# Windowed differential attention in a fused eight-layer kernel: fewer steps ahead of the unit loop, the rest as one piece per unit, and the copy of PV's result one unit later

## What is computed

```python
q = q * cos + rotate_half(q) * sin          # 16 heads
k = k * cos + rotate_half(k) * sin          # 4 heads, repeated 4 times
q1, q2 = (q[..., :SUB], q[..., SUB:])
k1, k2 = (k[..., :SUB], k[..., SUB:])
a1 = jnp.einsum('bhqd,bhkd->bhqk', q1, k1) * scale
a2 = jnp.einsum('bhqd,bhkd->bhqk', q2, k2) * scale
allowed = (col <= row) & (col >= row - WINDOW + 1)
...
p1 = jax.nn.softmax(a1 + neg, axis=-1)
p2 = jax.nn.softmax(a2 + neg, axis=-1)
diff = jax.nn.relu(p1 - lam[None, :, None, None] * p2)
diff = diff / (diff.sum(axis=-1, keepdims=True) + 1e-06)
out = jnp.einsum('bhqk,bhkd->bhqd', diff, v)
return out @ Wo
```

## Time and profile before

| | us |
|---|---|
| median of 3 runs | 1175.34 |
| lowest and highest | 1174.21 and 1176.25 |
| the profiled execution, device time | 1174.16 |
| its span in the trace | 1172.4 |
| rotated rows and spreads ahead of the loop | about 267.2 to 327.3 |
| the loop, first exponential to the last unit's POOL work | 327.3 to 455 |

### The profile page before, as it was taken

The page is one execution under the profiler, slowest core; times in us unless marked ns, Lnnn a source line. Parts: engine busy times, 40 slices in busy tenths (PEclk is TensorE's granted clock), DMA queues, the critical chain, the costliest instruction groups (busy, mean ns, idle before and its releaser), DMA issues. The chain is left out here.

```text
span 1172.4 us, 16450 instructions
## 1 busy us (share of the span) xinstructions
PE 1013.2 (86%) x5922; PEld 573.8 (49%) x5922; DVE 698.8 (60%) x1984; ACT 541.1 (46%) x1145; POOL 331.8 (28%) x464
## 2 busy tenths in 40 slices
PE   6999998787888886899999899997777988888785
PEld 2545455673344454436537444444454544445575
DVE  1667773775266784632431567778282588876665
ACT  3566655330488874210110456664304355555422
POOL 3312122330067874000000321112361054532222
PEclk8989998898767785899999899999767899999898
DMA  6000000103000000200000011000000000000000
GB/s 228 1 1 1 1 1 1 50 1 159 1 18 2 2 2 1 106 0 1 1 0 1 1 46 63 2 1 1 1 0 1 1 1 1 1 1 1 1 18 19
DMA packets 4325, 21.61 MB, mean 18 GB/s; under 512 B 377, under 2 KB 1657, under 8 KB 3220
## 3 DMA queue, kind: packets, MB, share of 16 engines
q1 hardware_dynamic: 4244, 20.55, 4.6%
HBM read 19.01 MB, written 1.05 MB: 17 GB/s over the span
## 5 line engine op out<-in xcount | busy, mean ns | idle before, releaser
L889 ACT ACTIVATE PB<-pair 128x1024 f32<-128x1024 f32 (+3 forms) x288 | 223.4, 811 | 135.0 <-PE pair L1603 133.4
L1129 DVE CUSTOM_DVE_ANT_0 junk<-bank,cst 128x128 bf16<-128x128 f32 (+3 forms) x384 | 171.2, 488 | 113.2 <-PE bank L1587 110.8
L725 POOL TENSOR_SCALAR_AFFINE_SELECT PB<-PB 128x256 f32<-128x256 f32 x192 | 79.0, 414 | 325.7 <-ACT PB L889 323.6
L1132 DVE TENSOR_REDUCE pmx<-bank 128x1 f32<-128x512 f32 x192 | 122.7, 685 | 51.6 <-PE bank L1587 50.7
L1587 PE MATMUL bank<-KO_r,QO_r 64*128 64x512 f32 (+3 forms) x576 | 139.6, 415 | 11.3 <-DVE A L1207 3.9
L1619 PE MATMUL pvb<-PB,V 128*32 128x512 f32 (+3 forms) x1152 | 124.7, 505 | 10.0 <-ACT PB L889 7.3
L1587 PEld LDWEIGHTS bank<-KO_r,QO_r 64*128 64x128 f32 x576 | 71.5, 189 | 113.4 <-DVE pmx L1129 40.1
L1599 PE MATMUL pair<-QO_r,KO_r 64*128 64x512 f32 (+3 forms) x576 | 114.8, 389 | 12.8 <-ACT PB L889 11.5
L731 POOL TENSOR_TENSOR parts_r<-y_f,parts_r 128x512 fp32r<-128x512 f32 x24 | 30.8, 1281 | 311.2 <-ACT parts_r L860 311.2
L1603 PE MATMUL pair<-ms,sel_r 64*128 64x512 f32 (+3 forms) x576 | 101.7, 345 | 0.0
L945 ACT ACTIVATE KO<-pair,nm 128x128 f32<-128x128 f32 x256 | 90.0, 402 | 23.4 <-DVE nm L1276 23.3
(11 more groups left out here) (205 smaller groups left out, 1697.6 us busy)
## 6 DMA issues: line engine op xcount, KB each, us to landing
WF<-in_moe_gu SPq DMA_DIRECT2D x1, 3520.0 KB, 10.8
WA<-in_w_att SPq DMA_DIRECT2D x3, 1024.0 KB, 9.8
WF<-in_tern_w SPq DMA_DIRECT2D x1, 3072.0 KB, 9.8
V<-in_moe_d SPq DMA_DIRECT2D x1, 1792.0 KB, 7.7
xT<-in_xT SPq DMA_DIRECT2D x2, 512.0 KB, 5.8
X<-in_x SPq DMA_DIRECT2D x1, 1024.0 KB, 10.6
A<-in_rope SPq DMA_DIRECT2D x1, 1024.0 KB, 4.7
out<-X SPq DMA_DIRECT2D x2, 512.0 KB, 2.9
```

Source lines behind the costliest of these rows:

```text
L725: pool.affine_select(p2, p2, pattern=[[0, 2], [1, P]], compare_op=ALU.is_ge, fill=0.0, base=0, channel_multiplier=-1).then_inc(causal, 1)
L889: act.activation(pb[:, st % 2, 2 * i:2 * i + 2, 0:n], ps[:, :, 0:n], ACT.Exp, scale=scale)\
L1129: r_done(dve.tensor_tensor_reduce(junk[:, (r_used - 1) % 3, 0:n], ps[:, 0:n], tri[:, HALF - n:HALF], 1.0, LOWEST, ALU.add, ALU.max, accum_ ...
L1132: r_done(dve.tensor_reduce(to, ps[:, 0:n], AX.X, ALU.max))
```

## The change

`W_BEFORE` keeps what unit 0 needs, and more items go into the loop. The column on the right is the loop after the change.

| | ahead of the loop, before | ahead of the loop, after | in the loop, after |
|---|---|---|---|
| R (rotated tiles) | 0 to 5 | 0 to 3 | 4 and 5, in two pieces each, units 4, 5 and 6, 7 |
| v | all tiles, last | half 1, behind R 0 | half 0 at unit 3 |
| spreads of k | 4 | 4 | |
| spreads of q, half 0 | 8 | 2 (group 0) | groups 1, 2, 3: two each at units 0, 1, 2 |
| spreads of q, half 1 | | | one each at units 8 to 15 (before: odd units 1 to 15) |

`rotate` and `tile_rows` handle one of the two products of a tile at a time; in the loop `middle(i)` stands behind the maxima and the ratio of the next unit. `middle(i - 1)` now stands behind the first product of `rotate(i)` and not behind the whole of it. `acc` moves one unit later on ACT (`pv` stays), `accT`, `outT`, `proj` and `norm` with it. `em`, a buffer of the last attention, has four places for two. The loop's new order around it is, by unit: `S0 s s | S1 s s | S2 s s | S3 v uT0 | S4 R uT1 | S5 R uT2 | S6 R uT3 | S7 R pv0 uT4 | S8 s acc0 uT5 | S9 s uT6 accT0 | ...`.

```diff
-W_E = ND + 12 + 2 * ND
+W_E = ND + 6 + 2 * ND
 ...
 def windowed_plan():
-    def rows(side, groups, half):
-        return [("s", side, g, x, half) for g in groups for x in range(TWO)]
-    before = [("R", 0), ("x1",), ("R", 1), ("R", 2), ("R", 3)] + rows("k", (0,), W_SOON) + rows("k", (0,), W_LATE) \
-        + rows("q", (0, 1), W_OUT) + [("R", 4)] + rows("q", (2, 3), W_OUT) + [("R", 5), ("v",)]
-    late = rows("q", range(NG), W_END)
+    def rows(side, g, half):
+        return [("s", side, g, x, half) for x in range(TWO)]
+    before = [("R", 0, 0), ("R", 0, 1), ("v", W_SOON), ("x1",)] + [("R", i, k) for i in (1, 2, 3) for k in range(2)] \
+        + rows("k", 0, W_SOON) + rows("k", 0, W_LATE) + rows("q", 0, W_OUT)
+    late = {0: rows("q", 1, W_OUT), 1: rows("q", 2, W_OUT), 2: rows("q", 3, W_OUT), 3: [("v", W_LATE)],
+            4: [("R", 4, 0)], 5: [("R", 4, 1)], 6: [("R", 5, 0)], 7: [("R", 5, 1)]}
+    for g in range(NG):
+        for x in range(TWO):
+            late[8 + TWO * g + x] = [rows("q", g, W_END)[x]]
     plan = []
     for k in range(len(UNITS) + 3):
         if k < len(UNITS):
             plan.append(("S", k))
-            if k % 2 and late:
-                plan.append(late.pop(0))
+            plan += late.get(k, [])
         else:
             plan.append(("flush", k))
         j = k - 3
+        if j > NG and j % NG == 1:
+            plan.append(("acc", j // NG - 1))
         if j >= NG and j % NG == 0:
-            plan += [("pv", j // NG - 1), ("acc", j // NG - 1)]
+            plan.append(("pv", j // NG - 1))
         if j >= 0:
             plan.append(("uT", j))
-        if j > NG and j % NG == 1:
+        if j > NG and j % NG == 2:
             plan.append(("accT", j // NG - 1))
-        step = j - NG * TH - 2
+        step = j - NG * TH - 3
         if 0 <= step < 8:
 ...
-        em = sb("em", [P, 2, NT, HG])
+        em = sb("em", [P, 4, NT, HG])
 ...
-                    sp.wait_ge(v_there, 1)
+                    sp.wait_ge(v_there, 2)
 ...
-            for i in range(len(W_HALVES)):
-                lowest(i)
+            for item in W_BEFORE:
+                if item[0] == "R" and item[2]:
+                    lowest(item[1])
             for item in W_PLAN:
+                if item[0] == "R" and item[2]:
+                    lowest(item[1])
                 if item[0] in ("S", "flush") and 1 <= item[1] <= len(UNITS):
 ...
-                    if item[0] == "R":
+                    if item[0] == "R" and item[2]:
                         highest(item[1])
                     if item[0] == "s":
                         act.activation(spread_to(item), e_slot()[:, :, :], ACT.Copy).then_inc(e_free, 1)
                 for item in W_PLAN:
+                    if item[0] == "R" and item[2]:
+                        highest(item[1])
                     if item[0] == "s":
                         n = w_banks(item)
 ...
-                def rotate(i):
+                def rotate(i, k):
                     tile, half = W_HALVES[i]
                     rows, sc = (P, SUB ** -0.5) if tile < 2 else (KV * HD, 1.0)
-                    cols = slice(half * HALF, (half + 1) * HALF)
                     x = w_buf[i % 2]
-                    if i >= 2:
+                    if i >= 2 and k == 0:
                         dve.wait_ge(w_lo, i - 1)
-                    for k in range(2):
-                        ps = r_slot()
-                        r_done(dve.scalar_tensor_tensor(x[0:rows, k, :], ps[0:rows, :], sc, rope[0:rows, k, cols],
-                                                        ALU.mult, ALU.mult))
+                    r_done(dve.scalar_tensor_tensor(x[0:rows, k, :], r_slot()[0:rows, :], sc,
+                                                    rope[0:rows, k, half * HALF:(half + 1) * HALF], ALU.mult, ALU.mult))
+                    if k:
+                        r_wait()
+                        dve.tensor_tensor(x[0:rows, 0, :], x[0:rows, 0, :], x[0:rows, 1, :], ALU.add).then_inc(w_rows, 1)
+                        turned.append(i)
+                def v_tiles(half):
+                    dve.wait_ge(w_blank, 1)
+                    dst = v_own[:, half * TH:(half + 1) * TH, :, 0:HD]
+                    r_done(dve.tensor_copy(dst, r_slot()[:, 0:TH * KV * HD].rearrange("p (t h d) -> p t h d", t=TH, h=KV)))
                     r_wait()
-                    dve.tensor_tensor(x[0:rows, 0, :], x[0:rows, 0, :], x[0:rows, 1, :], ALU.add).then_inc(w_rows, 1)
-                    dve.wait_ge(w_rows, i + 1)
+                    dve.nop().then_inc(v_there, 1)
 ...
+                turned = []
                 for item in W_BEFORE:
                     if item[0] == "R":
-                        i = item[1]
-                        rotate(i)
-                        if i:
-                            middle(i - 1)
+                        rotate(*item[1:])
+                        if item[2] == 0 and turned:
+                            middle(turned.pop())
                     if item[0] == "v":
-                        middle(len(W_HALVES) - 1)
-                        ps = r_slot()[:, :].rearrange("p (t h d) -> p t h d", t=NT, h=KV)
-                        last = dve.tensor_copy(v_own[:, :, :, 0:HD], ps)
-                        r_done(last)
-                        r_wait()
-                        dve.nop().then_inc(v_there, 1)
+                        v_tiles(item[1])
+                        middle(turned.pop())
+                middle(turned.pop())
                 for item in W_PLAN:
                     if item[0] == "S":
                         k = item[1]
@@ -1278,6 +1290,12 @@
                                               AX.X, ALU.max, negate=True).then_inc(wmax_ready, 1)
                     if item[0] in ("S", "flush") and 1 <= item[1] <= len(UNITS):
                         ratio(item[1] - 1)
+                    if item[0] == "S" and turned:
+                        middle(turned.pop())
+                    if item[0] == "R":
+                        rotate(*item[1:])
+                    if item[0] == "v":
+                        v_tiles(item[1])
 ...
-                def tile_rows(i):
+                def tile_rows(i, k):
                     tile, half = W_HALVES[i]
-                    rows, at = ((P, (tile * P, D + tile * P)) if tile < 2 else (KV * HD, (2 * D, 2 * D + KV * HD)))
+                    rows, at = ((P, tile * P + k * D) if tile < 2 else (KV * HD, 2 * D + k * KV * HD))
                     x_ready(half)
-                    for k in range(2):
-                        w = w_att(s, at[k], rows)
-                        ps = r_slot()
-                        over_width(ps[0:rows, :], lambda c: w[:, c, :],
-                                   lambda c: xT[:, c, half * HALF:(half + 1) * HALF]).then_inc(r_full, 1)
+                    w = w_att(s, at, rows)
+                    ps = r_slot()
+                    over_width(ps[0:rows, :], lambda c: w[:, c, :],
+                               lambda c: xT[:, c, half * HALF:(half + 1) * HALF]).then_inc(r_full, 1)
+                def v_tiles(half):
+                    w = w_att(s, 2 * D + 2 * KV * HD, KV * HD)
+                    x_ready(half)
+                    ps = r_slot()
+                    for k in range(TH):
+                        t = half * TH + k
+                        last = over_width(ps[:, k * KV * HD:(k + 1) * KV * HD], lambda c: xT[:, c, t * P:(t + 1) * P],
+                                          lambda c: w[:, c, :])
+                    last.then_inc(r_full, 1)
 ...
                 for item in W_PLAN:
+                    if item[0] == "R":
+                        tile_rows(*item[1:])
+                    if item[0] == "v":
+                        v_tiles(item[1])
 ...
-                            pe.wait_ge(v_there, 1)
+                            pe.wait_ge(v_there, 2)
```

More of the change, by code:

```diff
@@ L466, in uses_of_r @@
     for item in W_BEFORE + W_PLAN:
-        n += {"R": 2, "v": 1, "uT": 1, "accT": 1, "outT": ND, "proj": 1}.get(item[0], 0)
+        n += {"R": 1, "v": 1, "uT": 1, "accT": 1, "outT": ND, "proj": 1}.get(item[0], 0)
         if item == ("uT", gi):
@@ L874, in attention @@
                             act.wait_ge(mp_ready, n + 1)
-                            act.activation(em[:, n % 2, ts, :], nm[:, n % 2, ts, :], ACT.Exp, scale=scale)\
+                            act.activation(em[:, n % 4, ts, :], nm[:, n % 2, ts, :], ACT.Exp, scale=scale)\
                                 .then_inc(em_ready, 1)
@@ L1195, in attention @@
                         else:
-                            e = em[:, STAGES.index((g, qh)) % 2, t0:t0 + TH, :]
+                            e = em[:, STAGES.index((g, qh)) % 4, t0:t0 + TH, :]
                             cnt = cst[:, C_CNT + t0:C_CNT + t0 + TH].unsqueeze(2).to_broadcast([P, TH, HG])
@@ L1674, in windowed @@
                     if item[0] == "R":
-                        tile_rows(item[1])
+                        tile_rows(*item[1:])
```

(9 more changed lines are left out.)

## The result

The changed kernel takes 1169.37 us (median of 5 runs, 1167.74 to 1170.22) against 1174.66 for the kernel before (5 runs). The ratio is 0.9949, with a 95% interval of 0.9938 to 0.9961: 5.3 us less by the medians, where 4.5 were forecast. A second series, beside the experiments, gave 0.9962 (0.9948 to 0.9977). The profiled execution took 1170.22 us around a span of 1168.5.

A forecast was written before the change was run, and what follows sets the result against it. ACT and PE together were taken to bound the loop, PE's clock deciding which. Lead 25.9 - (22.8 + 24.8 - 30.7) - (36.9 - 33.0) - 0.6 = 4.5 us less: median 1170.8 us, range 1167 to 1174.

The forecast's parts named there:

- The start: Ahead of the loop: unit 0's exponentials start at 301.4 instead of 327.31, a lead of 25.9 us.
- Units 0 to 3: Loop start: each next unit waits for a spread behind all exponentials; 7.6 us each, 22.8 in all.
- Units 3 to 8: Loop units with v's second half and four products on PE, taken as mostly fast: 24.8 us.
- Units 8 to 16: Loop units with one spread each, half slow clock, half fast: 36.9 us against 33.0 before.
- rival 1: PE's fast clock holds behind the loop's start; units 8 to 16 take 32.5 us, median 1161; chance 0.16.
- The acc move: ACT's copy of PV's result a unit later: saves nothing, costs two times 0.4 us, 0.6 more at unit 16.
- the place of accT, outT, proj and norm: These steps a unit later in the loop: between -0.9 and +0.9 us, from the norm's wait on DVE; taken 0.
- units 16 to the end, the same work: 0: Rest of the sublayer from unit 16: same work as before, so no change, 0 us.
- Rival 2: Slow clock holds in the loop and PE becomes the bound: median 1186; chance 0.26 with halfway cases.
- rival 3: Start moves, but work is paid later and POOL, late by two lowest parts, takes the rest: 1175; chance 0.16.

The follow-up runs named there:

- e3: Changed kernel with the six spreads of q groups 1 to 3 of half 0 back ahead of the loop: 1164.98 us, 0.993 of the kernel before.
- e10: Changed kernel with q group 1 ahead of the loop too and v's second half by tiles in the gaps of units 1 and 2: 1164.87 us, 0.9906.
- e4: Changed kernel with rotated tiles 4 and 5 and v's second half back ahead of the loop, q spreads left in it: 1175.59 us, 0.9997.
- e7: e6 with tile 4's first product cut into unit 2's two gaps, the other three products at units 3, 4 and 5: 1170.99 us, 0.9982.
- e2: Kernel before with only the acc move (acc, accT, outT, proj and norm a unit later): 1170.62 us against 1173.27, 0.9974.
- e5: Changed kernel with only ACT's copy of PV's result back in PV's unit; accT, outT, proj, norm stay a unit later: 1166.86 us, 0.9959.
- e11: e9 with ACT's copy of PV's result back in PV's unit, accT, outT, proj and norm a unit later: 1165.34 us, 0.9916.
- e1: Changed kernel with the acc move undone: acc back in PV's unit, accT, outT, proj and norm a unit sooner: 1172.04 us, 0.9985.
- e6: Changed kernel with v's second half cut into four tiles, one in each PE gap of units 0 and 1: 1166.07 us, 0.9929.
- e8: e3 with PV of the first two tiles computed twice, 16 more dense matmuls each in units 7 and 11: 1165.58 us, 0.9913.
- e9: e3 with tile 5's products at units 8 and 10 and the eight spreads at units 7, 9 and 11 to 16: 1164.38 us, 0.9904.

## Why the prediction was right, and where it was not

The forecast by its own sum, 4.5 us less, stands beside 5.3 us in the first series and 4.5 in the second (by its ratio). The first half of the loop went much as it was written down. That the whole did too is partly luck, as the last terms show.

- *The start.* 25.9 us sooner forecast, 26.6 measured from the sublayer's first product. ACT's first copies at 291.8 and 291.71, the first exponential at 301.4 and 300.94. v's first half lay in PE's idle time as said, 2.00 us from 271.01.
- *Units 0 to 3.* 22.8 us forecast, 22.7 measured, at the slow clock (0.50; the forecast had 0.56), by the chain that was written down. e3 and e10 confirm its price by removing it: without the spreads three units take 8.2 us (e3). The kernel before took 9.1 there; the 3.8 a unit of the forecast is a mean over eight units.
- *Units 3 to 8.* 24.8 forecast, 25.3 measured, but not by the terms: unit 3 took 6.56 for 5.6 and unit 4 6.13 for 4.6, since PE stayed slow through v and most of the first product; units 5 to 7 took 4.53, 3.74 and 4.32 for 4.8, 4.5 and 5.3. The clock of the stretch, 0.79, was as said (near 0.8), with PE busy throughout.
- *Units 8 to 16.* 36.9 forecast, 37.1 measured in one profile and 34.0 in the other. The term rests on a mixture of two clocks, and the mixture is not the same in every execution. The slow end was good: 41.7 us at 0.50 in e4 and e7, which is the forecast's 6 x 4.75 + 2 x 6.6 without the 1.3 that it added for `acc`. The fast end was not added up rightly: rival 1's 32.5 us do not follow from its terms, 6 x 3.75 + 2 x 3.9 + 0.8 = 31.1. No run shows this stretch with eight spreads at 1.00.
- *The acc move.* This is the step that failed. I gave the move 1.4 us of cost, 0.8 in units 8 to 16 and 0.6 at unit 16, and the later accT, outT, proj and norm 0. Alone the move is worth 0.0026, 3 us (e2). For the copy the runs show no gain, as I had it, and no cost either (e5 and e11, within some 2 us). Wrong was the other part: the place of accT, outT, proj and norm, taken as 0 with 0.9 either way.
- *The rest of the change.* Without the move my sum gives 5.9 us (4.5 + 1.4); e1 measured 0.0015, 1.8 us, with an interval of 0 to 3.6. In its trace 4.3 us were there at unit 16, 1.6 fewer than 5.9, and 2.9 of them went in units 20 to 24. So two errors of some 4 us had opposite signs: the move, 1.4 us of cost for 3 of gain, and the rest, 5.9 us for 1.8. Of the second, "units 16 to the end, the same work: 0" is the larger part by that one trace. That they cancelled was luck.
- *The rivals.* Rival 2's mechanism is real, an all-slow stretch in which PE sets the pace (e4, e7), but it did not decide the changed kernel. Rival 1 shows in part in its second profile, 0.85 and 34.0 us; that everything behind unit 3 runs fast came in neither (0.79 in units 3 to 8, with PE never idle). The condition of rival 3, POOL's wait for the middle part, came (2.16 and 1.23 us ahead of L787 in units 5 and 7), with no loss behind it.

What stays open. That the move is worth some 3 us is shown by e1 and e2, and e5 and e11 put it on the place of the followers (accT, outT, proj and norm), within some 2 us; how it works is not shown. Single profiles cannot tell, as executions of one kernel differ by as much: units 16 to 31 took 60.0 us in the changed kernel and 63.7 in e1, but 62.6 in e2 and 63.5 in e5, both of which have the followers late too. Units 20 to 31, from exponential to exponential, took 43.1 to 43.2 us in seven profiles with copy and followers late (both of the changed kernel, e3, e4, e6, e7, e10), but 46.5 and 46.6 in e8 and e9, which have both late too, and 44.8 in e2. They took 46.1 to 46.6 in e1, e5 and e11 with the copy early, and 43.7 in the kernel before, which has it early as well. So neither place fixes whether these 3 us are lost. Why PE's granted clock rises in one arrangement and not in another is open as well. More dense products in units 8 to 16 went with a higher clock than e3's in e8 and e9, and products that ended by unit 5 or stood ahead of the loop went with 0.50 in e7 and e4, one profile each.

## What to carry to other kernels

Count what a step costs where it lands, not only what it frees: 26.6 us of earlier start left 5.2 after sixteen units. The largest part, 13.6 us, went in three units: a unit that needs the result of a step standing in the loop just ahead of it loses the overlap of two buffers (7.56 us a unit for 3.0). Look for the gaps that such a chain leaves, here 1.2 us each, and cut a piece of other work to fit them (e6), or pay for the chain once ahead of the loop (e3, 4.3 us faster than the changed kernel; e9 and e10 are no slower). When PE sets the pace, compare stretches with their granted clock beside them, over several executions and up to the end of the loop, or a profile's 3 to 7 us will be taken for the effect of an edit.

## What the runs showed of the hardware

- PE can be busy without a pause and stay at the lower of its two clock levels, 1.2 GHz: 43.00 of 43 us in e4 at a granted clock of 0.50, in a mixture of 64-row matmuls, spreads, transposes and PV. Units 8 to 16 took 27.5 us at 1.00 (e2, with four of the eight spreads), and with all eight 34.0 at 0.85, 37.1 at 0.68, 40.8 at 0.54 and 41.7 at 0.50.
- The clock is not fixed by the program. Two executions of the changed kernel agree within 0.1 us up to unit 8 and then run at 0.68 and 0.85; e4's and e7's times fall in two groups, some 8 and 4 us apart, the faster group each time at the higher clock of the whole execution (0.901 to 0.902 against 0.883 to 0.891, and 0.893 to 0.896 against 0.889 to 0.891).
